# Adding the old rows in the returned-results sum: an identity product on TensorE in place of additions on GpSimd

## The reference, cut to what matters

```
x = x + _L1_gnn_ref(_layernorm(x), adj, ...)
x = x + _L1_ffn_ref(_layernorm(x)[None], ...)[0]
...
out[row] = sum over its two experts of  gate * expert(row)   (+ gate * bias of the experts)
```

## Time and profile before

| what | us |
|---|---|
| median of three runs | 3156.52 |
| lowest and highest | 3156.28, 3159.9 |
| the profiled execution: its own time | 3158.89 |
| the profiled execution: first to last instruction (span) | 3157.1 |

### The profile page before, as it was taken

The page is one execution under the profiler, slowest core; times in us unless marked ns, Lnnn a source line. Parts: engine busy times, 40 slices in busy tenths (PEclk is TensorE's granted clock), DMA queues, the critical chain, the costliest instruction groups (busy, mean ns, idle before and its releaser), DMA issues. The chain is left out here.

```text
span 3157.1 us, 52623 instructions
## 1 busy us (share of the span) xinstructions
PE 2438.4 (77%) x18539; PEld 2039.5 (65%) x18539; DVE 1574.7 (50%) x3095; ACT 1142.8 (36%) x2211; POOL 553.1 (18%) x862
## 2 busy tenths in 40 slices
PE   6979599679957758855785999998989999844255
PEld 4858499579936634644784777777777777734153
DVE  3646412222236631143445677777677777732355
ACT  2333122012213211122213666656566656614421
POOL 0000122122212100420001111212112211120044
PEclk8999699789969969976897999999999999967587
DMA  4000022134231102720565231324244452021075
GB/s 124 1 7 1 26 84 90 63 96 143 75 96 64 35 27 87 243 81 22 220 266 155 74 105 35 91 87 130 66 136 128 115 142 64 18 57 38 8 230 190
DMA packets 147048, 293.48 MB, mean 93 GB/s; under 512 B 37154, under 2 KB 74056, under 8 KB 143716
## 3 DMA queue, kind: packets, MB, share of 16 engines
q1 hardware_dynamic: 127988, 237.43, 24.3%
q0 software_dynamic: 18800, 52.69, 6.1%
HBM read 488.56 MB, written 65.74 MB: 176 GB/s over the span
## 5 line engine op out<-in xcount | busy, mean ns | idle before, releaser
L2224 PE MATMUL tx_ring<-g_ident,tx_p 128*128 128x128 f32 x2552 | 394.6, 283 | 74.1 <-DVE tx_p_t L2464 35.8
L2224 PEld LDWEIGHTS tx_ring<-g_ident,tx_p 128*128 128x128 f32 x2552 | 286.2, 141 | 176.8 <-DVE tx_p_t L2464 58.6
L2464 DVE COPY tx_p_t<-tx_ring 128x512 f32<-128x512 f32 x464 | 305.6, 685 | 132.3 <-PE tx_ring L2224 129.7
L2457 DVE TENSOR_REDUCE tx_neg_max<-tx_scores 128x1 f32<-128x1354 f32 x232 | 362.0, 1561 | 16.1 <-PE tx_scores L2212 16.1
L2354 ACT ACTIVATE tx_p<-tx_scores,tx_neg_max 128x1354 f32<-128x1354 f32 x232 | 322.9, 1392 | 87.3 <-DVE tx_neg_max L2457 84.7
L2361 ACT ACTIVATE tx_p_t<-tx_ring 128x384 f32<-128x384 f32 x232 | 113.7, 490 | 294.8 <-PE tx_ring L2224 290.9
L2212 PE MATMUL tx_scores<-tx_keys,tx_queries 96*128 96x512 f32 (+1 forms) x696 | 202.2, 399 | 16.3 <-DMA tx_queries<-tx_q_hi 11.2
L2264 PE MATMUL tx_ring<-tx_p_t,tx_values 128*32 128x128 f32 x5104 | 174.2, 298 | 14.7 <-ACT tx_p_t L2361 12.8
L2264 PEld LDWEIGHTS tx_ring<-tx_p_t,tx_values 128*32 128x32 f32 x5104 | 156.3, 121 | 28.2 <-ACT tx_p_t L2361 24.0
L192 PE MATMUL ln_turned<-g_ident,g_xn 128*128 128x128 f32 x176 | 39.5, 409 | 138.3 <-DVE g_xn L179 138.3
L2212 PEld LDWEIGHTS tx_scores<-tx_keys,tx_queries 96*128 96x128 f32 x696 | 115.3, 193 | 27.5 <-issue 17.1
(11 more groups left out here) (910 smaller groups left out, 5265.2 us busy)
## 6 DMA issues: line engine op xcount, KB each, us to landing
tx_keys<-expert_keys SPq DMA_DIRECT2D x696, 169.5 KB
lv1e_w<-in_L_ffn_W SPq DMA_DIRECT2D x232, 256.0 KB
tx_w<-in_L_ffn_W SPq DMA_DIRECT2D x58, 1024.0 KB
lv0e_w<-in_L_ffn_W SPq DMA_DIRECT2D x200, 256.0 KB
tx_values<-expert_values SPq DMA_DIRECT2D x58, 704.0 KB
tx_rows<-in_L_ffn_rows SPq DMA_DIRECT2D x29, 640.0 KB, 3.7
sro_we<-_L_ffn_expert_out_weight SPq DMA_DIRECT2D x29, 512.0 KB, 5.5
nee_w<-in_L_ffn_w SPq DMA_DIRECT2D x58, 256.0 KB, 4.1
```

The lines of the kernel that those rows point to most:

```text
L2224: last = nc.tensor.transpose(ring[u % 2][:, (t - t0) * P:(t - t0 + 1) * P], p[n % 2][:, t * P:(t + 1) * P], g.ident[:])
L2457: nc.vector.tensor_reduce(neg_max[:, n % 4:n % 4 + 1], sc[n % 2][:, 0:N], AX_X, ALU.max, negate=True)\
L2464: nc.vector.tensor_copy(p_t[:, n % TURNED, t0:t0 + nt, :], ring[u % 2][:, 0:nt * P].rearrange("p (t q) -> p t q", q=P))\
```

## The change

`sum` is gone, with its buffer `with_second` and the semaphores `second_done` and `summed`. `spread` starts, in the four adding stages, with a product of the identity and the block's old rows of `g.x` into the block's bank, on which the product of biases then accumulates. It uses all eight banks of PSUM in place of four, in all five stages, and calls `late` ahead of the last two banks, which waits until the tiles' work has read them. The old rows' products of the first eight blocks stand ahead of the waits for the table. `mix` writes `second` straight to `g.x`.

```diff
@@ four stages, GpSimd's list @@
-            back.sum(pool)
@@ shared and routed; the others likewise @@
-            back.spread(pe, spare)
+            back.spread(pe, spare + turned + row, lambda eng: eng.wait_ge(y_done, tiles))
-            back.mix(dve, spare)
+            back.mix(dve, spare + turned + row)
@@ attention @@
+            def ring_read(eng):
+                for who in drained:
+                    eng.wait_ge(drained[who], sum(1 for e, _ in after if e == who))
+
+            back.spread(pe, spare + ring, ring_read)
@@ class Returns @@
+    def spread(self, pe, banks, late):
+
+        def old(b):
+            n = rows_of(b)
+            if b == len(banks) - 2:
+                late(pe)
+            self.nc.tensor.matmul(banks[b % len(banks)][:, 0:D], self.g.ident[0:n, :], self.acc[0:n, b, :], start=True, stop=False)
+
+        def bias(b):
+            if b == len(banks) - 2 and not self.add:
+                late(pe)
+            self.nc.tensor.matmul(banks[b % len(banks)][:, 0:D], self.plan.coef_t[:, b * P:(b + 1) * P], self.table[:],
+                                  start=not self.add, stop=True).then_inc(self.row_full, 1)
+
+        if self.add:
+            for b in range(len(banks)):
+                old(b)
         pe.wait_ge(self.table_loaded, 16)
         if self.pads:
             pe.wait_ge(self.pads_loaded, 16)
         for b in range(NB):
             if b >= len(banks):
                 pe.wait_ge(self.first_done, b + 1 - len(banks))
+                if self.add:
+                    old(b)
+            bias(b)
...
-            if self.add and b >= 2:
-                dve.wait_ge(self.summed, b - 1)
...
-            into = self.with_second[0:n, b % 2, :] if self.add else self.acc[0:n, b, :]
-            self.nc.vector.scalar_tensor_tensor(out=into, ...).then_inc(self.second_done, 1)
+            self.nc.vector.scalar_tensor_tensor(out=self.acc[0:n, b, :], ...)
-
-    def sum(self, pool):
-        for b in range(NB):
-            n = rows_of(b)
-            pool.wait_ge(self.second_done, b + 1)
-            self.nc.gpsimd.tensor_tensor(self.acc[0:n, b, :], self.acc[0:n, b, :], self.with_second[0:n, b % 2, :],
-                                         ALU.add).then_inc(self.summed, 1)
```

More of the change, by code:

```diff
@@ L1565, in __init__ @@
         self.table_dram, self.pads = table_dram, plan.experts if pads else 0
-        self.table, self.with_first, self.with_second = lent or (
-            s.sb("ret_table", [plan.width, D]), s.sb("ret_first", [P, 2, D]), s.sb("ret_second", [P, 2, D]))
+        self.table, self.with_first = lent or (s.sb("ret_table", [plan.width, D]), s.sb("ret_first", [P, 2, D]))
         self.table_loaded, self.row_full = s.sem("ret_table_loaded"), s.sem("ret_row_full")
-        self.first_done, self.second_done, self.summed = s.sem("ret_first_done"), s.sem("ret_second_done"), s.sem("ret_summed")
+        self.first_done = s.sem("ret_first_done")
         self.fetched = [s.sem(f"ret_fetched{c}") for c in range(CH)]
@@ L1622, in mix @@
             dve.wait_ge(self.first_done, b + 1)
-            into = self.with_second[0:n, b % 2, :] if self.add else self.acc[0:n, b, :]
-            self.nc.vector.scalar_tensor_tensor(out=into, in0=self.g.made[0:n, b, 1, :],
+            self.nc.vector.scalar_tensor_tensor(out=self.acc[0:n, b, :], in0=self.g.made[0:n, b, 1, :],
                                                 scalar=self.plan.share[0:n, b, 1:2], in1=self.with_first[0:n, b % 2, :],
-                                                op0=ALU.mult, op1=ALU.add).then_inc(self.second_done, 1)
-    def sum(self, pool):
-        for b in range(NB):
-            n = rows_of(b)
-            pool.wait_ge(self.second_done, b + 1)
-            self.nc.gpsimd.tensor_tensor(self.acc[0:n, b, :], self.acc[0:n, b, :], self.with_second[0:n, b % 2, :],
-                                         ALU.add).then_inc(self.summed, 1)
+                                                op0=ALU.mult, op1=ALU.add)
 W1_PARTS = 4
@@ L1738, in _ @@
             back.load_pads(pool)
-            if add:
-                back.sum(pool)
         @block.tensor
@@ L1788, in _ @@
                     second(i - 1)
-            back.spread(pe, wide)
+            back.spread(pe, wide + turned + row, lambda eng: eng.wait_ge(y_done, tiles))
         def free_hidden(eng, i):
@@ L1834, in _ @@
             result(tiles - 1)
-            back.mix(dve, wide)
+            back.mix(dve, wide + turned + row)
 def stage_keys_values(nc, g, a, plan):
@@ L2067, in stage_attend_tiles @@
         sc = [s.ps(f"scores{i}", [P, CH * BANK]) for i in range(2)]
-        spare = [sc[k][:, c * BANK:(c + 1) * BANK] for k in range(2) for c in range(2)]
+        spare = [sc[k][:, c * BANK:(c + 1) * BANK] for k in range(2) for c in range(CH)]
         ring = [s.ps(f"ring{i}", [P, BANK]) for i in range(2)]
-        back = Returns(nc, g, s, plan, g.x, a["L2_ffn_be2"], True, lent=(wq[0:plan.width, 0, :], tmp, x1_r))
+        back = Returns(nc, g, s, plan, g.x, a["L2_ffn_be2"], True, lent=(wq[0:plan.width, 0, :], tmp))
         x_loaded = [g.s.sem(f"tx_x_loaded{i}") for i in range(2)]
@@ L2571, in _ @@
                             inverse(i, 1)
-            back.mix(dve, spare)
+            back.mix(dve, spare + ring)
         @block.gpsimd
@@ L2796, in _ @@
                 second(i)
-            back.spread(pe, spare + wide)
+            back.spread(pe, spare + wide + turned + row, lambda eng: eng.wait_ge(y_done, tiles))
         @block.scalar
@@ L2869, in _ @@
                 normalise(i)
-            back.mix(dve, spare + wide)
+            back.mix(dve, spare + wide + turned + row)
 def normalised_experts(nc, g, a):
```

6 lines of the change are left out of this document (removed).

## The result

The changed kernel takes 3118.5 us (median of four runs, 3117.3 to 3122.1) against 3156.4 for the kernel before on the same chip (also four runs): ratio 0.988, 95% interval 0.9863 to 0.9897, so 37.9 us less. Forecast were 3127 us and a range of 3120 to 3138. One execution of the kernel before, on the chip of the first experiments, took 5716.7 us, far beyond all others, and is in no comparison. The profiled execution took 3119.2 us with a span of 3117.5.

What follows compares the result with a forecast made beforehand. At the five stage ends the last engine to finish was taken as the bound, GpSimd in the four that add. 4 x 7.4 = 29.6 us (29.5 with second decimals) off the median of 3156.5 gave 3127 us, range 3120 to 3138.

Steps and rivals of the forecast that it cites:

- The four items of the gap: Landing to barrier, adding stages against `lv0e`: pace 1.5, last `second` 0.2, last addition 0.8, GpSimd's drain 4.9; 7.4 us a stage.
- pace, last `second` and last addition: At the adding stages' ends: gain from removing GpSimd's additions themselves, 2.5 us a stage, 10 us in all.
- The drain's length: GpSimd's drain, moved behind the sends in adding stages, would last 4.2 to 4.9 us, hidden by load and mix.
- The Trainium skill's rule against the step: VectorE's port lock could hold GpSimd's drain through the mix: 10 us gained, not 29.5; drain-stays rival's chance 7%.
- TensorE's cost of nothing: Old rows' products in the four adding stages would not delay the mix: 0, at most 1.5 us in `sro`.
- The blocks behind each stage keep their own length, measured from the barrier: Program behind each of the five stages keeps its length, so only the returns' gains count.
- the rival that I gave the stages behind: Granted clock falls otherwise in stages behind: more than 6 us either way, 3117 to 3121 or 3134 to 3140; 5%.
- the clock's rival: Granted clock differs in the unedited stages from each norm on, which begin 7 to 22 us earlier; chance 5%.

Runs made afterwards that it cites:

- the first experiments: The first four follow-up runs, all on one chip, not that of the result; the kernel before took 3164.0 us there.
- early drain: Kernel before, with one GpSimd drain put ahead of its additions, which stay on GpSimd; ratio 0.9942 to the kernel before.
- late drain: Changed kernel, with GpSimd held back in the four adding stages until the last `first` is made, ahead of its closing drain; ratio 0.9941 to the kernel before.
- four banks: Changed kernel with four PSUM banks for the products in place of eight; ratio 0.9978 to the kernel before.
- the five profiles without the added instructions: Profiles of the kernel before (three), of it with a GpSimd drain ahead of the additions, and of the changed kernel with VectorE adding the old rows.
- the eight with them: Profiles of programs with the added TensorE instructions: the changed kernel three times, and five follow-up kernels that contain the identity products.
- the discarded products: Kernel before, its four adding returns beginning with the 11 identity products, overwritten by the bias products; GpSimd adds as before; 3156.3 against 3163.1 us.
- the two repeats: Changed kernel, unchanged, measured again on two later chips: 3127.5 us (ratio 0.9888) and 3128.0 us (ratio 0.9889) to the kernel before.

## Why the prediction was right, and where it failed

- *The four items of the gap*: right, each. They gave the forecast's 29.6 us. Line 1635 takes 485 ns in all five; no addition follows VectorE; the drain stands behind the sends. Moving the drain alone either way moves the returns by 4.8 and 4.5 us (early and late drain); what is left after the early drain, 12.9 - 10.3 = 2.6 us, is the 2.5 us forecast for pace, last `second` and last addition.
- *The drain's length*: forecast as 4.2 to 4.9 us; it is 4.8 to 4.9 in the adding stages, since their 29 tiles bring 58 or 59 indirect DMAs against 51 in `lv0e`. No price changed by it, as it is hidden.
- *The Trainium skill's rule against the step* ("SBUF — State Buffer", section "SBUF: two separate sides", on GpSimd's descriptors and VectorE's locks) was hardly put to the test: in the kernel after every closing drain is over at least 0.7 us before its mix. The late drain's begins 0.3 us before the last `second` ends, and has its 4795 ns all the same.
- *TensorE's cost of nothing*: right, but its prices were off in both directions. The first 16 bias instructions of `lv1e` took 7.0 us (878.6 to 885.5) where 7.5 were forecast, the 12 of the last three blocks also 7.0 (885.5 to 892.4) where 5.6 were. So the last block had 0.9 us to spare, where 1.1 or more was forecast: partly luck. `lv1e` is the tightest, and not `sro`, which had 1.6 us; four banks lost all.
- *The failed step* is "The blocks behind each stage keep their own length, measured from the barrier", and with it the rival that I gave the stages behind. I let these stages change by the granted clock alone, and priced the 88 products only by the time that they run. What they also did was to lengthen TensorE's program, so that two packets of it no longer fall beside two weight loads. The two stages give 2.0 and 2.1 us on the mean of the five profiles without the added instructions and the eight with them (84.8 to 82.8, 19.6 to 17.4). Of these 4.1 us the earlier landings are 2.7. The other 1.4 lie behind TensorE's start, where the granted clock differs.
- *The sum now*: 29.6 + 4.1 = 33.7 us, a ratio of 0.9893. It lies within all three intervals (0.9863 to 0.9897, 0.9866 to 0.991, 0.9874 to 0.9904), where the forecast's 0.9907 lies in the second alone. The remaining 1.4 to 4.2 us of the medians are not settled; the discarded products too gave 6.8 us where the two stages give 4.1, so that more packets than these two may matter, in places that I didn't find. The measured 3118.5 us lies in the band of the clock's rival (3117 to 3121), but of its more than 6 us the two stages show 1.4, part of which follows from the earlier loads, and the clock's part in `tx` was chance of one profile. That the time fell outside the range at all is partly chance too: the 35.2 and 35.1 us of the two repeats, taken from 3156.5, would lie 1.3 us inside it.

## What to carry to other kernels

Before pricing an engine's removed work, read its drain at the end of the block: GpSimd's closing drain grew here with the indirect DMAs since its last drain. Work put behind the sends exposed it, and an early drain hid it. Whatever adds or removes instructions on TensorE can move the fetches of its program, and a stage that starts with a small load can win or lose 2 us by that; a control that only discards the new work shows it. Eight banks in place of four decided here whether a second product per block is free or costs the whole gain.

## What the runs showed of the hardware that I had not expected

- GpSimd's drain, when all sends have landed, costs some 82 ns for each indirect DMA since the last drain (21, 51, 58 and 59 DMAs: 1.77, 4.22, 4.79 and 4.87 us), the same 15.5 us later. In the midst of the sends 37 DMAs cost 4.6 to 4.8 us. Behind one large casting load it takes 22 us.
- TensorE's program, as the counts have it, comes in 16 KB packets over the DMA engines during the run, about one for 256 instructions. A packet of 1.1 to 1.8 us beside an 8 KB load nearly doubled its 1.7 us to 3.2, and put 1.3 us on a load of 1 MB. The granted clock then rose 3.3 us later in that stage, which cost another 1.0 us.
- At the low clock a product of old rows and one of biases, in turn into one bank, start 1.15 us apart, where bias products into fresh banks one after the other start 0.84 us apart (878.56 to 881.91 for four).
